# An attention and mixture-of-experts layer on one core: the third step's gate clamp ahead of its normalisation, and the last batch's router exponentials and norm scales moved

## The reference

```python
q, k, v = x @ Wq, x @ Wk, x @ Wv          # 16 query heads, 4 key/value heads, 128 wide
# softmax attention on rotated q, k (causal)
y = softmax(rope(q) @ rope(k).T * 128 ** -0.5, causal) @ v
# gated linear attention: S is a 128x128 state per head
S = S * exp(log_sigmoid(k_t) / 16) + softmax(k_t)[:, None] * v_t[None, :]
o_t = softmax(q_t) @ S
x = layernorm(x + (0.5 * y + 0.5 * o) @ Wo)
# router: 8 experts, the 2 best per token, weighted by softmax(x @ gate_w.T)
x = layernorm(x + sum(w_e * (silu(x @ w_gate[e]) * (x @ w_up[e])) @ w_down[e]))
```

## Time and profile before

| | |
|---|---|
| median of 3 runs | 963.8 us (962.95 to 964.1) |
| profiled execution: its own time | 969.53 us |
| profiled execution: span | 967.7 us |
| mean granted TensorE clock | 0.985 |
| busy: PE, DVE, ACT, POOL | 912.3, 666.7, 662.3, 634.7 us |

### The profile page before, as it was taken

The page is one execution under the profiler, slowest core; times in us unless marked ns, Lnnn a source line. Parts: engine busy times, 40 slices in busy tenths (PEclk is TensorE's granted clock), DMA queues, the critical chain, the costliest instruction groups (busy, mean ns, idle before and its releaser), DMA issues.

```text
span 967.7 us, 18183 instructions
## 1 busy us (share of the span) xinstructions
PE 912.3 (94%) x5091; PEld 703.6 (73%) x5091; DVE 666.7 (69%) x1982; ACT 662.3 (68%) x2138; POOL 634.7 (66%) x609
## 2 busy tenths in 40 slices
PE   7899999999999999999999999999999989998991
PEld 4677777777778787877777777777777766776770
DVE  4777767686767676778676969676978674451284
ACT  6677777777777777776777767776768674454562
POOL 6868685767565657677767768776658882536352
PEclk9899999999999999999999999999999999999996
DMA  7101100000000000800000000010102111223363
GB/s 256 34 17 34 40 1 1 6 13 7 1 0 0 0 0 6 263 6 1 1 2 1 2 6 6 2 63 2 63 1 74 53 57 55 84 89 120 106 202 113
DMA packets 34072, 43.30 MB, mean 45 GB/s; under 512 B 3772, under 2 KB 27966, under 8 KB 33856
## 3 DMA queue, kind: packets, MB, share of 16 engines
q1 hardware_dynamic: 30240, 33.83, 11.6%
q0 software_dynamic: 3744, 8.43, 2.5%
HBM read 25.65 MB, written 18.43 MB: 46 GB/s over the span
## 4 chain that ended last, share of the span: by engine, by line
PE 70%; DVE 11%; ACT 8%; issue 7%; DMA 2%; POOL 1%; DVEq 0%; SPq 0%; ACTq 0%; POOLq 0%; another core or an unknown queue 0%
PE MS L567 10%; PE OA L594 9%; PE PR L481 9%; PE S L576 7%; PE S L548 7%; PE S L693 5%; PE OA L710 4%; PE OA L556 4%; DVE S L999 3%; ACT eqk L824 3%; PE PR L521 3%; PE OA L587 3%; PE PR L527 2%; DMA acc<-in_x_rows 1%; DVE rq_lo L1109 1%
## 5 line engine op out<-in xcount | busy, mean ns | idle before, releaser
L1498 POOL TENSOR_TENSOR qd<-eqk,eg 128x512 f32<-128x512 f32 x63 | 74.9, 1189 | 154.6 <-issue 149.3
L594 PE MATMUL OA<-wT,V 128*128 128x512 f32 x320 | 149.6, 598 | 0.0
L786 ACT ACTIVATE S<-S,nm 128x128 f32<-128x128 f32 (+3 forms) x256 | 127.2, 497 | 9.3 <-DVE nm L999 8.3
L999 DVE CUSTOM_DVE_ANT_0 S<-S,maskb 128x128 f32<-128x128 f32 (+3 forms) x256 | 118.2, 519 | 14.9 <-PE S L548 11.3
L824 ACT ACTIVATE eqk<-qkv,nmx 128x128 f32<-128x128 f32 x320 | 125.1, 398 | 3.7 <-DVE nmx L1074 3.7
L1486 POOL TENSOR_TENSOR eqk<-eqk,rse 128x640 f32<-128x640 f32 x63 | 79.6, 1264 | 56.8 <-DVE rse L1117 35.5
L594 PEld LDWEIGHTS OA<-wT,V 128*128 128x128 f32 x320 | 59.8, 191 | 68.9 <-issue 68.9
L1033 DVE TENSOR_TENSOR pr<-S,rl 128x256 f32<-128x256 f32 (+3 forms) x128 | 105.5, 825 | 4.5
L1475 POOL TENSOR_TENSOR rp<-qkv,cos 128x640 f32<-128x640 f32 x64 | 99.5, 1555 | 6.5 <-ACT qkv L814 5.3
L1478 POOL TENSOR_TENSOR rp<-rp,rt 128x640 f32<-128x640 f32 x64 | 99.7, 1557 | 5.0
L1475 POOL TENSOR_TENSOR rt<-qkv,sin 128x640 f32<-128x640 f32 x64 | 99.2, 1551 | 0.0
(11 more groups left out here) (173 smaller groups left out, 2496.0 us busy)
## 6 DMA issues: line engine op xcount, KB each, us to landing
qkv<-slot_x SPq DMA_DIRECT2D x46, 129.0 KB
pr<-plane SPq DMA_DIRECT2D x16, 256.0 KB
gu_w<-in_wgu SPq DMA_DIRECT2D x8, 352.0 KB, 3.4
slot_x<-zero SPq DMA_DIRECT2D x2, 1290.0 KB, 8.4
stage<-in_wqkv SPq DMA_DIRECT2D x6, 384.0 KB, 3.6
xraw<-in_x_cols SPq DMA_DIRECT2D x16, 128.0 KB, 2.5
acc<-in_x_rows SPq DMA_DIRECT2D x1, 2048.0 KB, 11.6
dn_w<-in_wdn SPq DMA_DIRECT2D x8, 256.0 KB, 4.2
```

Of the source, the lines that this page charges most:

```text
L594: last = pe.matmul(OA[:, :], V[:, j, :], wT[:, j, :], start=(c == 0 and j == 0), stop=(j == c))
L786: nc.scalar.activation(S[:, h, 0:n], S[:, h, 0:n], ACT.Exp, bias=nm[:, h:h + 1], scale=-1.0, accum_out=ls[:, h:h + 1]).then_inc(s_exp, 1)
L999: nc.vector.tensor_tensor_reduce(out=S[:, h, 0:n], in0=S[:, h, 0:n], in1=maskb[:, N - n:N], scale=-1.0, scalar=FAR, op0=ALU.add, op1=ALU.m ...
```

## The change

Five edits. (1) `clamp_gates` of the next chunk stands ahead of both normalisations in the steps c == 1 and c == 2, before only in c == 1. (2) In the very last attention step the probabilities are transposed first and the two slot tiles turned behind them, on TensorE and on ScalarE, and ScalarE loads the table with Silu ahead of that. (3) `router_exp(3)` goes from round 11 to the end of the last round (NT + 1 = 47), between a load of the table with Exp and one of the table with Sqrt. (4) `route_weigh(1)` goes from round 17 to behind the rounds, ahead of the combination of the last batch. (5) The last batch's two powers on GpSimd are replaced by a square root on ScalarE (`deviations`) and a reciprocal on VectorE in `shift2`.

```diff
@@ TensorE, step @@
+                turn_weights(g, c)
                 if not n1:
                     turn_x(0)
                     turn_x(1)
-                turn_weights(g, c)
@@ ScalarE, step @@
                 if not n1:
-                    x_out(0)
-                    x_out(1)
+                    act.preload_act_table_set("silu_and_others")
                 if first and c:
                     act.wait_ge(s_splo, 3 if c == 1 else 4)
                 weights_out(g, c)
+                if not n1:
+                    x_out(0)
+                    x_out(1)
@@ ScalarE @@
+            def deviations(i):
+                v, r = (x[:, 2 * i:2 * i + 2] for x in (ve[2], rstd[2]))
+                act.wait_ge(s_ve[2], i + 1)
+                nc.scalar.activation(r, v, ACT.Sqrt).then_inc(s_rs[2], 1)
@@ ScalarE, rounds @@
-                if q == 11:
+                if q == NT + 1:
+                    act.preload_act_table_set("natural_log_exp_and_others")
                     router_exp(3)
+                    act.preload_act_table_set("sqrt_and_others")
                 if q >= 40:
                     norm2(q - 40)
             for t in range(NT + 2 - 40, TILES - 1):
+                if t in (3 * TPB, 3 * TPB + 2):
+                    deviations(t // 2)
                 norm2(t)
@@ VectorE, step @@
-                if n1 and c == 1:
+                clamp_first = c in (1, 2)
+                if n1 and clamp_first:
                     clamp_gates(g, c + 1)
                 normalise(g, c, 0)
-                if n1 and c != 1:
+                if n1 and not clamp_first:
                     clamp_gates(g, c + 1)
                 normalise(g, c, 1)
@@ VectorE, shift2 @@
                 dve.wait_ge(s_rs[2], 2 * n + h + 1)
+                if n == 3:
+                    nc.vector.reciprocal(rstd[2][:, i], rstd[2][:, i]).then_inc(s_rc, 1)
+                    dve.wait_ge(s_rc, h + 1)
@@ VectorE, rounds @@
-                if q == 17:
-                    route_weigh(1)
...
             shift2(2, 1)
+            route_weigh(1)
@@ GpSimd @@
             rs2(2, 1)
-            rs2(3, 0)
-            rs2(3, 1)
```

More of the change, by code:

```diff
@@ L264, in layer_kernel @@
         s_mark, s_back, s_bf = sem("s_mark"), sem("s_back"), sem("s_bf")
-        s_last = sem("s_last")
+        s_last, s_rc = sem("s_last"), sem("s_rc")
         s_yg = [sem(f"s_yg{i}") for i in range(4)]
```

## The result

The changed kernel's median is 952.85 us (950.79 to 953.34, 4 runs), beside 963.38 us (961.72 to 964.1, 4 runs) for the kernel before on the same chip. The ratio is 0.9889, with a 95% interval of 0.9869 to 0.9909: faster by 10.5 us, interval 8.8 to 12.6. The forecast was 8.0 us and 955.8 us. The profiled execution took 953.34 us (span 951.5). One of the nine runs of the kernel before that the last four experiments are compared with took 1045.6 us at a mean granted clock of 0.842, and the ratios leave it out.

A forecast was written before the change was run, and what follows sets the result against it. TensorE, holding 70% of the chain that ended last, was taken as the bound; 6.45 + 0.9 - 0.5 + 0 + 1.0 + 0.1 = 7.95 us, taken as 8.0 off 963.8, gave 955.8 us, range 952.8 to 960.0.

The forecast's parts named there:

- Part 1: Third attention steps: the clamp ahead of the normalisation saves 0.43 us per step, 15 x 0.43 = 6.45 us.
- The bound of the second normalisation: Third steps: the transposes cannot start before the second normalisation ends, so they gain at most 0.45 us per step.
- that of the projection's end: Third steps: the output product cannot start before the projection ends, so it gains at most 0.43 us per step.
- Rival 1: ScalarE's chain takes back Part 1's gain inside each group: 962.3 us in full (chance 0.05), 959.0 by half (0.10).
- rival 2: Third steps: GpSimd's decay blocks the second normalisation beside it, making the kernel slower, 975.2 us; chance 0.04.
- Rival 4: TensorE does not wait for the clamp, and tables load more often than written: about 963.8 us; chance 0.03.
- Part 2: Last group's third step: the earlier clamp lets the transposes start sooner, 0.9 us gained.
- Part 3: Last attention step: turning the first two slot tiles behind the weights' transposes loses 0.5 us; early silu table load 0.
- two clock cases: Clock stays up in Part 2: 954.7 us; it also falls in Part 3: up to 957.5. Chance with forecast 0.75.
- Part 4: Round 11: moving the router exponential and its table load out gains 1.0 us, bounds 0.7 and 1.3.
- Part 5: Tail behind the last tile: moved router work is covered, GpSimd's power replaced; net 0.1 us gained, bounds 0.3 either way.
- more than forecast: Whole kernel: the gain exceeds the forecast; chance 0.03.

The follow-up runs named there:

- the last four experiments: The changed kernel with slot tiles turned first (950.87 us), with eight unused matmuls (952.69 us), with the clamp first in fourth steps (948.76 us), with turns and clamp edits together (947.96 us).
- the late power: The changed kernel with one more GpSimd power of 128x2 behind the last variance, its result unread: 956.15 us.
- the best one: The changed kernel with the slot tiles turned first again and the clamp ahead in the second, third and fourth steps: 947.96 us.
- the unused matmuls: The changed kernel with eight matmuls on zeros in TensorE's idle time ahead of the last step's transposes: 952.69 us.

## Why the prediction was right, and where it was not

**Part 1** was right in mechanism and nearly in size. Forecast 0.43 us per step, measured 0.40: 6.1 us in 14 groups, less the 0.5 us that kernels without this edit show there too. The bound of the second normalisation is met in the timeline above; that of the projection's end was not strict, by 0.16 us, and did not decide. It isn't the same in every group: the third step is shorter by 0.41 to 0.45 us in eleven of the fourteen, by 0.56 in the first and by only 0.22 and 0.31 in the last two, for which no run here shows the reason. Rival 1, that each group loses it again, and rival 2, that the decay blocks the normalisation, are both ruled out by the run with the clamp alone (7.9 us, interval 6.8 to 9.4, where rival 1 in full leaves nothing of part 1, by half leaves at most 5.2 us with the clock up, and rival 2 makes the kernel slower) and by the 0.96 us of the normalisation beside the decay. On that point the rule cited in the prediction (the Trainium skill, SBUF — State Buffer, SBUF: two separate sides) agrees with the trace. Rival 4, that the clamp was not what TensorE waited for, falls with the same run.

**Part 2** had the right sign, and its clock case came out the good way. I took 0.9 and kept 1.1 for the clock outside the sum. The transposes took 1.53 us at the upper clock instead of 2.61, and the step gained 2.0. With part 1's 15 x 0.40 = 6.0 that makes 8.0 us, against 7.9 for the kernel with the clamp alone.

**Part 3** was the sum's weak term. The order itself was forecast to cost 0.5 and costs 0.43. The clock I took at 0, with "up to 1.7 us" as the bound, and it cost 1.66. I argued from the clock having stayed up in this place, but after a wait of 1.78 us, while the change makes that wait 2.20. The two clock cases that I had named separately both happened, and that they nearly cancel (+1.1 and -1.7) is luck, not foresight. What the prediction said of the turns' old place holds too: the slots land later than TensorE arrives, the turns wait for them (until 803.13 and 803.71 with the turns first again), and the wait for the normalisation covers that, since the last step is as long as before, 13.60 us.

**Part 4** was right: forecast 1.0, measured 0.99 in the profile, 1.2 in time. The table load took 1.28 us with the exponential 0.02 us behind it, so the Trainium skill's figure for a switch (ScalarE: Activation LUTs, What ACT_TABLE_LOAD costs), cited in the prediction, again does not fit this trace, and its sum (1.38 us more) was not seen.

**Part 5 is the step that failed.** It was forecast at 0.1 us net, and measured at 3.1 to 3.3. The working of the chain was right: from the last `ve` to the last norm it takes 0.84 us and not 1.17, and 0.20 of that is lost to the first half's reciprocal. The sentence that failed is "GpSimd's queue loses two operations that nothing else waits for". The end of the program waits for them: GpSimd's closing DRAIN ends 6.5 us behind its last operation, and SyncE's queue with the last store only 3.0 us behind the start of the last norm. It stood in the trace of before, in the closing lines, at 960.3 with 7.2 us, and the span's end lay 3.4 us behind the end of SyncE's DRAIN. I read the chain that ended last up to the last norm at 961.26 and took what lies between it and the span's end (6.4 us) for a constant. The listing of that chain even passes through GpSimd's closing line, with 0.74 us at 960.30.

**The sum.** By the terms as measured: 6.0 + 2.0 - 2.1 + 1.0 + 3.2 = 10.1 us, against 10.5 measured (interval 8.8 to 12.6). That is 2.15 us more than the forecast's 7.95: 3.1 more from part 5 and 1.1 from part 2, 1.6 less from part 3 and 0.45 less from part 1. The kernel before is 963.38 us in these runs and 963.8 in those that I started from, which is another 0.4 us of the distance from 955.8. The result, 952.85 us, lies at the very low end of the range of 952.8 to 960.0 and outside the 953.5 to 957.5 that the forecast with its clock cases was given: neither had a term for an end of the program that moves by 3 us, and "more than forecast" had been given a chance of 0.03.

## What to carry to other kernels

A small operation that others queue behind should stand as soon as its input is there, if what releases the tensor engine hangs on it: here 0.28 us of work moved past 1.1 us is worth 0.4 us in nearly every group, and the fourth step had another 0.17 us to give. Read the end of the program too, each engine's closing instructions and not only the last useful one: what is on GpSimd near the end can set the end though nobody reads it. And before moving work out of a gap of TensorE, add up the gap that is left and ask what clock the matmuls behind it will have.

## What the runs showed of the hardware

GpSimd's closing DRAIN ended 6.4 to 6.5 us behind its last tensor operation in all ten profiles, among them before (961.03 to 967.5), changed (937.45 to 943.9), only the clamp (947.02 to 953.5) and with the late power (948.20 to 954.7). The other engines' DRAINs are far shorter: VectorE's takes 0.52 us, ScalarE's 0.63 and TensorE's 1.0 to 2.0. The Trainium skill (VectorE: DVE Perf Modes, The DRAIN you can't avoid) speaks of DRAINs of the program's frame that are constant at about 12 ns on all five engines. SyncE's 7 ns is near that, GpSimd's 7.2 to 8.4 us is not, and the measurement decides. What it waits for is not shown.

The granted clock doesn't follow from the length of one wait. TensorE waits for GpSimd's `qd` near 769 us in the last attention groups: 2.00 us with the clamp in the fourth step, 2.03 us in the changed kernel and 2.07 us in the best one, and the clock fell behind it; 2.03 us with the clamp alone, 2.04 us with the turns first again and 2.07 us with the unused matmuls, and it stayed up. Behind the wait of 2.20 to 2.22 us in the last step it fell in all three profiles that have it (changed, late power, clamp in the fourth step), and behind 1.36 to 1.78 us there it stayed up in the six others without unused matmuls. One execution each: how often it falls in the runs without a profile stays open, and the spread of the runs of one kernel (950.79 us at a mean granted clock of 0.991, 953.34 at 0.985, for the changed one) is larger than the 1.7 us that one such stretch costs.
